# A two-block vision network on one core: inverse norms by Newton steps on VectorE, a new order of the first pass, and a middle stage image by image

## The reference

```python
# L0 conv: shifted-window attention, 12 heads of 8 channels, windows of 64 tokens
qkv = xw @ qkv_w.T + qb
qn = q / jnp.maximum(jnp.linalg.norm(q, axis=-1, keepdims=True), 1e-12)
kn = k / jnp.maximum(jnp.linalg.norm(k, axis=-1, keepdims=True), 1e-12)
attn = jnp.einsum('whid,whjd->whij', qn, kn) * scale + bias      # then mask, softmax, @ v, @ proj
# L0 ffn: two layers with sign weights, outputs clipped by the largest value of each group of images
h = _bitlinear(x, W1, b1)        # clip(y * QB / (gamma + EPS)), gamma = max |y| over 3 images
h = jax.nn.gelu(h, approximate=False)
out = _bitlinear(h, W2, b2)
```

## Time and profile before

| | |
|---|---|
| median of 3 runs | 1477.58 us (1475.88 to 1477.93) |
| the profiled execution: its own time | 1476.25 us |
| its span, first to last instruction | 1474.5 us |
| first pass, first layer norm to last reduction | 343.4 us (50.5 to 393.9) |
| middle stage | 47.8 us (396.2 to 444.0) |
| last stage | 1030.5 us (444.0 to 1474.5) |
| busy over the span | PE 976.5, DVE 763.3, ACT 597.5, POOL 401.3 us |
| TensorE's granted clock, mean | 0.760 of full speed; 0.75 in the first pass, 0.78 in the middle stage |
| DMAs of x in the first pass, issue to landing | 1.8 to 2.1 us |

### The profile page before, as it was taken

The page is one execution under the profiler, slowest core; times in us unless marked ns, Lnnn a source line. Parts: engine busy times, 40 slices in busy tenths (PEclk is TensorE's granted clock), DMA queues, the critical chain, the costliest instruction groups (busy, mean ns, idle before and its releaser), DMA issues.

```text
span 1474.5 us, 26072 instructions
## 1 busy us (share of the span) xinstructions
PE 976.5 (66%) x8998; PEld 671.1 (46%) x8998; DVE 763.3 (52%) x2165; ACT 597.5 (41%) x1259; POOL 401.3 (27%) x525
## 2 busy tenths in 40 slices
PE   0266667666564434677777877767777878767876
PEld 0154555554343233354464563554544645534454
DVE  1156666555342444476465564564754655645342
ACT  0255556555351011433444425334334444254542
POOL 3377777776001021211111212111111112111000
PEclk9987676767585555787786886887877878878776
DMA  3000000000000100000000000000000000000000
GB/s 96 9 10 11 10 9 11 9 9 7 6 0 16 26 24 22 24 13 22 23 6 25 15 19 25 15 19 25 9 21 25 8 25 15 19 23 4 4 3 3
DMA packets 51853, 24.46 MB, mean 17 GB/s; under 512 B 37977, under 2 KB 49802, under 8 KB 51818
## 3 DMA queue, kind: packets, MB, share of 16 engines
q1 hardware_dynamic: 51818, 24.01, 6.5%
HBM read 16.10 MB, written 7.88 MB: 16 GB/s over the span
## 4 chain that ended last, share of the span: by engine, by line
PE 24%; issue 18%; DVE 11%; ACT 9%; POOL 3%; DMA 1%; DVEq 0%; SPq 0%; ACTq 0%; POOLq 0%
PE ps L1240 20%; ACT stackt L1042 3%; DVE nm L920 3%; DVE xs L899 2%; DVE samp L896 2%; ACT prob L1198 1%; PE ps L1245 1%; ACT L1198 1%; POOL srstd L516 1%; POOL hatr L592 1%; PE ps L1543 1%; DVE th L880 1%; DVE hat L881 1%; ACT th L1152 0%; ACT hb L1224 0%
## 5 line engine op out<-in xcount | busy, mean ns | idle before, releaser
L1042 ACT COPY stackt<-ps 128x768 bf16<-128x768 bf16 x192 | 142.8, 829 | 92.2 <-PE ps L1245 92.1
L1240 PE MATMUL ps<-stackt 53*64 53x64 bf16 (+3 forms) x2304 | 111.3, 247 | 87.5 <-ACT stackt L1042 50.6
L1240 PE MATMUL ps<-b_xnt,we 128*128 128x256 f32 x384 | 143.5, 494 | 2.6 <-ACT hb L1224 2.3
L1224 ACT ACTIVATE hb<-ps 128x512 f32<-128x512 f32 (+1 forms) x128 | 63.1, 493 | 202.3 <-PE ps L1240 202.1
L552 POOL TENSOR_TENSOR rn<-ss,neghalf 128x24 f32<-128x24 f32 x32 | 132.7, 4163 | 42.1 <-DVE ss L749 42.1
L920 DVE TENSOR_REDUCE nm<-ps 128x2 f32<-128x512 f32 x192 | 120.5, 685 | 30.1 <-PE ps L1240 26.9
L1198 ACT ACTIVATE prob<-ps 128x512 f32<-128x512 f32 x192 | 104.2, 594 | 63.9 <-PE ps L1240 63.8
L1240 PEld LDWEIGHTS ps<-stackt 53*64 53x64 bf16 (+3 forms) x2304 | 49.1, 115 | 170.8 <-issue 58.8
L516 POOL TENSOR_TENSOR prstd<-pveps,neghalf 128x2 f32<-128x2 f32 x48 | 42.5, 885 | 309.8 <-DVE pveps L709 302.5
L1240 PEld LDWEIGHTS ps<-we,hb 128*128 128x128 f32 x768 | 110.7, 220 | 26.0 <-ACT hb L1224 20.5
L1240 PE MATMUL ps<-we,hb 128*128 128x96 f32 x768 | 111.8, 303 | 15.8 <-ACT hb L1224 15.8
(11 more groups left out here) (229 smaller groups left out, 1676.4 us busy)
## 6 DMA issues: line engine op xcount, KB each, us to landing
rows<-xn_scratch SPq DMA_DIRECT2D x96, 48.0 KB, 1.9
hatst<-hat_scratch SPq DMA_DIRECT2D x96, 48.0 KB, 2.1
xn_scratch<-xnp SPq DMA_DIRECT2D x48, 48.0 KB, 1.8
hat_scratch<-hatp SPq DMA_DIRECT2D x16, 144.0 KB, 1.9
xraw<-x_scratch SPq DMA_DIRECT2D x16, 96.0 KB, 2.0
out<-acc SPq DMA_DIRECT2D x16, 96.0 KB, 1.8
we<-in_we SPq DMA_DIRECT2D x1, 768.0 KB
xin<-in_x SPq DMA_DIRECT2D x16, 48.0 KB, 1.8
```

The lines of the kernel that those rows point to most:

```text
L1042: return a.copy(stackt[:, x, :, P * t:P * t + P], bank_bf(bank))
L1224: a.activation(hb[:, e % 2].rearrange("p m n -> p (m n)")[:, 2 * TOK * k:2 * TOK * k + n_], ps[:, 6, 0:n_], ACT.Gelu).then_inc(S("c_h"), 1)
L1240: return m.matmul(o, l, r, start=start, stop=stop)
```

## The change

The first pass: the two POOL instructions that make `rn` are gone. DVE makes `rn` in step p3 instead, for both tiles at once: a shift and a subtraction on the bits of the sum give a first guess of the inverse root, and three Newton steps of three instructions each refine it. DVE's wait for POOL's `rn` is gone from step r1. `ORDER_A` is another string with the same letters, so that on every engine the steps stand in another order.

The middle stage: no hardware loop and no groups. Fifteen images are written out one behind the other, with three buffers in `hb` (an image waits for the product three images back), four PSUM banks, and DVE's largest value two images behind its clip.

```diff
-ORDER_A = "afafpfaafprfrarpp"
+ORDER_A = "apfaffapfrarpfapr"
+HBUFS = 3
+YBANKS = 4
+BLAG = 2
...
             def project_a(i):
...
-                w("qk", 0)
-                w("ss", 1)
-                for t in range(TILES):
-                    g.tensor_tensor(rn[:, t].rearrange("p a h -> p (a h)"), ss[:, t, :], neghalf[:, 0:2 * HEADS],
-                                    ALU.pow).then_inc(S("a_rn"), 1)
+                for t in range(TILES):
                     yield
...
                 w("sq", 2)
+                w("qk", 0)
                 own.link(v.tensor_reduce(ss[:], sq[:].rearrange("p t a h c -> p t (a h) c"), AX.X, ALU.add))
-                v.tensor_scalar(ss[:], ss[:], 1e-24, None, ALU.max).then_inc(S("a_ss"), 1)
+                flat = lambda x: x.rearrange("p a b -> p (a b)")
+                sums, root, half = flat(ss[:]), rn[:].rearrange("p t a h -> p (t a h)"), flat(rh[:])
+                own.link(v.tensor_scalar(sums, sums, 1e-24, None, ALU.max))
+                own.link(v.tensor_scalar(root.bitcast(I32), sums.bitcast(I32), 1, None, ALU.arith_shift_right))
+                own.link(v.tensor_scalar(root.bitcast(I32), root.bitcast(I32), -1.0, float(0x5F3759DF), ALU.mult, ALU.add))
+                for _ in range(3):
+                    own.link(v.scalar_tensor_tensor(half, root, -0.5, root, ALU.mult, ALU.mult))
+                    own.link(v.tensor_tensor(half, half, sums, ALU.mult))
+                    own.link(v.scalar_tensor_tensor(root, half, 1.5, root, ALU.add, ALU.mult))
...
                 for t in range(TILES):
-                    w("rn", t + 1)
                     own.link(v.tensor_tensor(rn[:, t, 0, :], rn[:, t, 0, :], lscale[:], ALU.mult))
...
-            with dve.Fori(1, GROUPS + 1) as i:
...
+            for n in range(QIMG + BLAG):
+                if n < QIMG:
+                    h0 = hb[:, n % HBUFS].rearrange("p m n -> p (m n)")
+                    if n >= HBUFS:
+                        w("y2", n - HBUFS + 1)
+                    own.link(v.tensor_scalar(h0, y1all[:, n].rearrange("p m n -> p (m n)"), qs1[:, n:n + 1], LIM, ALU.mult, ALU.min))
                     v.tensor_scalar(h0, h0, -LIM, None, ALU.max).then_inc(S("b_cl"), 1)
...
+                if n >= BLAG:
+                    w("y2_sb", n - BLAG + 1)
...
-            with act.Fori(1, GROUPS + 1) as i:
...
+            for n in range(QIMG + 1):
+                if n < QIMG:
+                    h0 = hb[:, n % HBUFS].rearrange("p m n -> p (m n)")
+                    w("cl", n + 1)
                     a.activation(h0, h0, ACT.Gelu).then_inc(S("b_h"), 1)
...
+                if n >= 1:
+                    y = n - 1
+                    w("y2", y + 1)
...
-            with pe.Fori(1, GROUPS + 1) as i:
...
+            for n in range(QIMG):
+                w("h", n + 1)
+                if n >= YBANKS:
+                    w("y2_sb", n - YBANKS + 1)
```

More of the change, by code:

```diff
@@ L32 @@
 BF16 = mybir.dt.bfloat16
+I32 = mybir.dt.int32
 ALU = mybir.AluOpType
@@ L261, in build_program @@
         signals("a_", "sp", x_in=48, x1_out=48)
-        signals("a_", "dve", var=1, xn=1, ss=1, qk=2, nm=2, prob=2, on=2, x1=1, var2=1, xn2=1, gm=1)
-        signals("a_", "pool", rstd=1, rn=2, va=1, split=1, rstd2=1)
+        signals("a_", "dve", var=1, xn=1, qk=2, nm=2, prob=2, on=2, x1=1, var2=1, xn2=1, gm=1)
+        signals("a_", "pool", rstd=1, va=1, split=1, rstd2=1)
         signals("a_", "act", xnt=1, sq=2, qkv_sb=2, v=1, copies=1, qt_sb=2, kt_sb=2, q2t_sb=2, exp=2, ot=1, ont=1,
@@ L267, in build_program @@
                 x2t=1, y1=1)
-        signals("b_", "dve", cl=GIMG, gm=GIMG)
-        signals("b_", "act", h=GIMG, y2_sb=GIMG)
-        signals("b_", "pe", y2=GIMG)
+        signals("b_", "dve", cl=QIMG, gm=QIMG)
+        signals("b_", "act", h=QIMG, y2_sb=QIMG)
+        signals("b_", "pe", y2=QIMG)
         signals("c_", "sp", x_in=16, xn_out=48, rows_in=96, hat_out=16, hat_in=96, out=16)
@@ L824, in _ @@
             gammas(0, gm1, qs1)
-            with dve.Fori(1, GROUPS + 1) as i:
[L826 to L833, removed]
+            own = Own(dve, "dve_first")
+            w = waits(dve, "b_", 1)
+            for n in range(QIMG + BLAG):
[4 more added lines that the diff above has]
+                    own.link(v.tensor_scalar(h0, y1all[:, n].rearrange("p m n -> p (m n)"), qs1[:, n:n + 1], LIM, ALU.mult, ALU.min))
                     v.tensor_scalar(h0, h0, -LIM, None, ALU.max).then_inc(S("b_cl"), 1)
-                for u in range(GIMG):
-                    img = bass.ds((i - 1) * GIMG + u, 1)
-                    w("y2_sb", u + 1)
-                    v.tensor_reduce(gm2[0:C, img], y2all[:, img, :].rearrange("p a n -> p (a n)"),
+                if n >= BLAG:
+                    w("y2_sb", n - BLAG + 1)
+                    v.tensor_reduce(gm2[0:C, n - BLAG:n - BLAG + 1], y2all[:, n - BLAG, :],
                                     AX.X, ALU.max, apply_absolute_value=True).then_inc(S("b_gm"), 1)
-            dve.wait_ge(S("b_gm"), (GROUPS + 1) * GIMG)
+            dve.wait_ge(S("b_gm"), 2 * QIMG)
             gammas(1, gm2, qs2)
@@ L1110, in _ @@
             run_pass(act, ORDER_A, BEHIND_A, p=project_a, r=split_a, a=attend_a, f=finish_a)
[L1112 to L1124 removed]
+            w = waits(act, "b_", 1)
+            roll = SHIFT * SIDE
+            for n in range(QIMG + 1):
+                if n < QIMG:
+                    h0 = hb[:, n % HBUFS].rearrange("p m n -> p (m n)")
+                    w("cl", n + 1)
+                    a.activation(h0, h0, ACT.Gelu).then_inc(S("b_h"), 1)
+                if n >= 1:
+                    y = n - 1
+                    w("y2", y + 1)
+                    a.activation(y2all[:, y, roll:TOK], ps[0:C, y % YBANKS, 0:TOK - roll], ACT.Identity, bias=b2[:, 0:1])
+                    a.activation(y2all[:, y, 0:roll], ps[0:C, y % YBANKS, TOK - roll:TOK], ACT.Identity,
                                  bias=b2[:, 0:1]).then_inc(S("b_y2_sb"), 1)
@@ L1370, in _ @@
             run_pass(pe, ORDER_A, BEHIND_A, p=project_a, r=split_a, a=attend_a, f=finish_a)
-            with pe.Fori(1, GROUPS + 1) as i:
-                w = waits(pe, "b_", i)
-                w("y2_sb", 0)
-                for u in range(GIMG):
-                    w("h", u + 1)
-                    for k in range(MT):
-                        ins = mm(ps[0:C, u, 0:TOK], w2s[:, k, :], hb[:, u, k, :], k == 0, k == MT - 1)
-                    ins.then_inc(S("b_y2"), 1)
-            pe.wait_ge(S("b_y2_sb"), (GROUPS + 1) * GIMG)
+            w = waits(pe, "b_", 1)
+            for n in range(QIMG):
+                w("h", n + 1)
+                if n >= YBANKS:
+                    w("y2_sb", n - YBANKS + 1)
+                for k in range(MT):
+                    ins = mm(ps[0:C, n % YBANKS, 0:TOK], w2s[:, k, :], hb[:, n % HBUFS, k, :], k == 0, k == MT - 1)
+                ins.then_inc(S("b_y2"), 1)
+            pe.wait_ge(S("b_y2_sb"), 2 * QIMG)
             def offsets_c(i):
```

13 lines of the change are left out of this document (2 added, 11 removed).

## The result

The changed kernel takes 1435.13 us, the median of 4 runs (1434.15 to 1440.78), against 1477.32 for the kernel before on the same chip: a ratio of 0.9724 with the interval 0.9697 to 0.975. The forecast was 1444 within 1430 to 1458. Its profiled execution was the slowest of the four, 1440.78 us with a span of 1438.8.

The account below looks back on a forecast made before the run. A cycle through all engines, with POOL's powers as its largest piece, was taken to bound the first pass. First pass 16.9 us less plus middle stage 16.4 less, 33.3 in all: about 1444 us for the median, range 1430 to 1458.

Parts of the forecast that it names:

- The bound: First pass: no engine is full; a cycle through all engines sets the turn, POOL's powers (8.29 us) its largest piece.
- the forecast's first part: First pass: POOL's powers go and DVE gets eleven small instructions instead, 2.64 us in all, bounds 2.1 and 3.9.
- The turn: First pass, DVE's queue walked from one copy to the next: 18.85 us a turn against 19.64.
- The Newton steps: DVE in the first pass: shift, subtraction and nine Newton instructions at 0.24 us each, 2.64 in all.
- Rival D: First pass: DVE's Newton steps and POOL's split delay each other, up to 3.9 us a turn, 1495 us; chance 0.03.
- The stall before prob: First pass, DVE: the new order makes it stand still 2.36 us a turn until ACT's exponential is done.
- The loop: First pass: each turn 0.79 us shorter, 10.3 us less in 13 turns.
- Filling: Start of the first pass: 8.29 us of powers give way to 2.64, statistics (1.20) come out; 4.4 us less.
- Draining: End of the first pass, first turn without p, sums' end to b_xn: 9.6 us becomes 7.4, 2.2 less.
- The middle stage: Images written out: first gm at 5.97, next 2.29 later, 13 steps of 1.75, 0.42; 31.4 us, 16.4 less.
- Rival B: The middle stage stays at half clock, 1451 us for the whole; chance 0.07.
- The last stage: Untouched and left as it is, 1030.5 us; a move of more than 2 us would mean the forecast is wrong.

Follow-up runs that it names:

- powers_after_split: The changed kernel with POOL's two powers back instead of DVE's Newton steps, both placed behind POOL's split: 1421.65 us, ratio 0.9623 to the kernel before.
- casts_late: The changed kernel with ACT's four bf16 casts of qk moved behind the exponential, squares and y1's move reordered too: 1432.93 us, ratio 0.9717 to the kernel before.
- newton_old_order: The changed kernel with the old ORDER_A, so Newton steps on DVE in the old order of steps: 1467.68 us, ratio 0.9928 to the kernel before.

## Why the prediction was right, point by point

- **The bound.** The cycle over all engines with POOL's powers in it was the bound of the first pass. powers_after_split refines this: the powers cost what they did because of where they stood in the order. They can stay on POOL in a turn of 17.24 us, so the forecast's first part, that they had to go, was not what the gain needed.
- **The turn.** Forecast 18.85, measured 18.53. All places agree within 0.26 us; the difference is the branch, 0.36 in the forecast and nothing measured. That gm stands so exactly in its place is in part luck: prob began 0.26 earlier than forecast, since the exponential came 0.25 earlier, and from the sums to gm it takes 3.82 us where I had 3.55.
- **The Newton steps.** 0.24 from one to the next, as forecast. Shift and subtraction have no price of their own: 0.19 each where POOL is idle, in the filling turns,

```profile
70.03 0.19 DVE L754 TENSOR_SCALAR rn<-ss 128x48 int32<-128x48 int32 x1
```

  but 0.37 at 214.05, beside POOL's last cast.
- **Rival D, DVE against POOL.** The Trainium skill (SBUF — State Buffer, section Who interferes with whom) has a VectorE instruction with two inputs in SBUF and a GpSimd one that reads SBUF lock each other out, for the whole of an instruction. The trace agrees once the pairs are taken apart, DVE's two products and POOL's first subtraction:

```profile
211.09 0.96 DVE L790 TENSOR_TENSOR prob<-prob,expbias 128x768 f32<-128x768 f32 x1 [2.19 <-ACT prob L1089]
211.97 1.31 DVE L790 TENSOR_TENSOR prob<-prob,expbias 128x768 f32<-128x768 f32 x1
```

```profile
211.24 1.22 POOL L542 TENSOR_TENSOR stack<-res,stack 128x192 bf16<-128x192 f32 x1
```

  The first product takes the 0.96 that it takes alone. The subtraction begun beside it needs 0.55 alone (in before, at 243.78) and ends 0.41 behind it; the second product ends 0.82 behind the subtraction, and the second subtraction (212.42, 1.26) again 0.4 behind the second product. These are nearly the steps of a product behind a product (0.87) and of a subtraction behind a subtraction (0.50), so each waited for the other's end. So D's condition was met, and its price wasn't: the two products take 2.18 instead of 1.83, the small instructions 0.28 more, some 0.6 us a turn on DVE instead of 3.9, while POOL's two subtractions take 2.44 instead of 1.05. The first three of POOL's six instructions (209.09 to 211.16) fall into DVE's stall before prob, all but the last 0.07 us, and POOL's own waiting costs nothing here.
- **The stall before prob.** Forecast 2.36, measured 2.19, released by the exponential. casts_late took 1.0 off it by moving the casts, and the turn gained only a third of that.
- **The loop.** Forecast 10.3 in 13 turns, measured 13.4 in the 12 turns from the first gm to the last one in the loop.
- **Filling.** Forecast 4.4, measured 3.2 up to the first gm.
- **Draining, the step that was mis-sized.** Forecast 2.2, measured 7.4. I counted one turn, up to b_xn. In the first draining turn the sums stood between gm and divide before (343.69 to 345.85, gm's start to the sums' end, 2.2 us) and are gone from there now; it went from 18.0 to 13.5 us, of which I had 2.2. And I gave nothing to the second, which has no powers at all. DVE before, and after:

```profile
361.71 0.95 DVE L804 TENSOR_REDUCE gm<-y1all 128x1 f32<-128x768 f32 x1 [4.43 <-ACT y1all L1105]
...
373.59 0.56 DVE L714 TENSOR_SCALAR b_xn<-xres,smv,srstd 128x96 f32<-128x96 f32 x2
379.53 0.95 DVE L804 TENSOR_REDUCE gm<-y1all 128x1 f32<-128x768 f32 x1 [5.37 <-ACT y1all L1105]
```

```profile
341.66 0.95 DVE L813 TENSOR_REDUCE gm<-y1all 128x1 f32<-128x768 f32 x1 [0.27 <-ACT y1all L1112]
...
351.64 0.57 DVE L715 TENSOR_SCALAR b_xn<-xres,smv,srstd 128x96 f32<-128x96 f32 x2 [0.81 <-POOL srstd L521]
...
356.69 0.95 DVE L813 TENSOR_REDUCE gm<-y1all 128x1 f32<-128x768 f32 x1 [0.97 <-ACT y1all L1112]
```

  Before, b_xn stood behind prob in DVE's queue, which waited for the exponential; in the new order b_xn starts as soon as srstd is there and prob's wait runs beside the ffn product. 17.8 us become 15.0.
- **The middle stage.** Forecast 31.4, measured 29.2. The start was right (5.97 and 2.29 in the forecast, 5.71 and 2.56 measured); the step was 1.58 in the mean of 13 instead of 1.75, and the whole lies below the 30.1 that I gave as its bound. I had taken DVE's own work as 1.65; its two clips and gm overlap to 1.45 where nothing waits. The steps are 1.45, 1.52 and 1.72 in turn, and the longest holds a wait of 0.18 for ACT. The clock was 0.86 for the stage, where I had named 0.9 or more, since its first 9 us were at 0.55. Rival B did not come.
- **The last stage.** The forecast left it untouched and named a move by over 2 us as a sign of error. It moved by 6.3 us, in code that the change doesn't touch, with the same instructions and a lower granted clock (0.74 against 0.75 in the mean); whether the stages ahead of it have a part in that is open. Without this the profiled run would have been 42 us faster instead of 35.7: the good agreement of the profiled run with the forecast (1438.8 against 1441.2) owes 6 us to it, and that is luck. By the stages the change was worth 24.0 + 18.6 = 42.6 us, where the forecast had 33.3, and the median of the four runs, 9 us below the forecast, says the same.
- **The attribution.** The forecast gave half of the gain to the first pass as a whole and did not ask what of it was the order and what the Newton steps. newton_old_order and powers_after_split answer this for the loop: the new order gives all of the gain there, provided that the powers are taken out of the split's way; Newton steps are one way to do that, moving the powers a cheaper one. Newton steps gain in filling in either order, and in draining only in the new one.

## What to carry to other kernels

Where a long instruction sits in a cycle, move it within its engine's queue before making it shorter on another engine: here the same powers, put behind the work that the next turn waits for, gave more than their replacement did. A replacement that adds work to the engine whose queue is the cycle is paid in full, once a turn; its gain shows only where the pipeline fills and drains. And a stage in short groups that end in a full stop lost twice, by the missing overlap and by the clock, which in groups was granted at 0.61 to 1.00 and image by image was 1.00 after the first 9 us: 51.0 or 47.8 us against 29.2.

## What the hardware showed beside this

The branch back of a hardware loop cost DVE nothing where its next instruction had no one to wait for: 0.87 us from gm's start to the next turn's copy, less than gm's own 0.95, and as long as behind the last turn of the loop. I had read 0.36 from the earlier trace rows, at the end of a pass that everyone waits for. A single-source instruction on 128 x 48 integers took 0.19 us alone and 0.37 beside a POOL cast. The second of two 128 x 768 products beside POOL's 128 x 192 subtractions took 1.31 us, alone 0.96, each waiting for the other's end. And in one execution of before a group of three images took 7.95 us at a granted clock of 1.00 and 10.57 at 0.68, with PE's burst at 4.12 and 6.74.
